# Graph network on one core: load and gather waits taken per pair of groups in the two network passes

## The reference, cut to what matters

```python
def _propagate(h, edge_attr, edge_index, We, be, Wl):
    x_i = h[edge_index[0]]
    x_j = h[edge_index[1]]
    x_edge = jnp.concatenate([x_i, x_j, edge_attr], axis=-1)
    x_edge = _mlp1(x_edge, We, be)          # silu(x @ We + be)
    x_edge = edge_attr @ Wl * x_edge
    x_p = _seg_mean(x_edge, edge_index[0], h.shape[0])
    return x_p + h
```

## Time and profile before

| | |
|---|---|
| median of 3 runs | 16204.83 us (16196.27 to 16240.02) |
| the profiled execution | 16222.93 us, its span 16221.2 us |
| POOL busy / PE busy / DVE busy | 9525.9 / 9592.5 / 7215.4 us (59% / 59% / 44%) |
| gathers of the two passes, first to last | 7210.7 to 13034.2 us |
| clock granted to TensorE, mean | 0.693 |

### The profile page before, as it was taken

The page is one execution under the profiler, slowest core; times in us unless marked ns, Lnnn a source line. Parts: engine busy times, 40 slices in busy tenths (PEclk is TensorE's granted clock), DMA queues, the critical chain, the costliest instruction groups (busy, mean ns, idle before and its releaser), DMA issues.

```text
span 16221.2 us, 180153 instructions
## 1 busy us (share of the span) xinstructions
PE 9592.5 (59%) x40895; PEld 6450.1 (40%) x40896; DVE 7215.4 (44%) x18628; ACT 3844.3 (24%) x8556; POOL 9525.9 (59%) x8465
## 2 busy tenths in 40 slices
PE   0466657766478878845555556655555545555555
PEld 0111122221133333335555554555555545555554
DVE  8876657777000000013333332333333357777776
ACT  0344444442011111112222222222222212222221
POOL 0378878888645434426666664566666645555553
PEclk9999999999688778865555555555555555555555
DMA  9922222222599989992222223222222344444444
GB/s 385 358 15 19 19 15 20 20 20 18 168 342 370 343 306 357 359 113 86 84 86 84 85 84 50 75 84 86 84 86 85 80 95 139 141 141 140 140 139 96
DMA packets 1483063, 2197.01 MB, mean 135 GB/s; under 512 B 882955, under 2 KB 926027, under 8 KB 1454669
## 3 DMA queue, kind: packets, MB, share of 16 engines
q1 hardware_dynamic: 907628, 1490.52, 28.2%
q0 software_dynamic: 453120, 343.50, 12.7%
q10 hardware_dynamic: 121698, 356.43, 6.0%
HBM read 1771.19 MB, written 419.98 MB: 135 GB/s over the span
## 4 chain that ended last, share of the span: by engine, by line
POOL 40%; DMA 22%; issue 21%; PE 8%; DVE 4%; another core or an unknown queue 3%; ACT 1%; POOLq 0%; SPq 0%; DVEq 0%; ACTq 0%
POOL gat L645 18%; POOL adj L613 12%; POOL arena L645 8%; DMA arena<-adj 8%; DMA gat<-q_table,ring_i 6%; DMA arena<-h_table,ring_i 5%; PE bank L1029 5%; DMA adj<-put_n,put_at 2%; POOL rec_src L599 1%; DVE arena L1356 1%; PE same L1161 1%; PE same L1000 1%; DVE arena L1358 1%; PE same L980 0%
## 5 line engine op out<-in xcount | busy, mean ns | idle before, releaser
L645 POOL DMA_INDIRECT gat<-q_table,ring_i x3456 | 3626.6, 1049 | 2405.7 <-DMA gat<-q_table,ring_i 1025.0
L613 POOL DMA_INDIRECT adj<-put_n,put_at x1632 | 2559.9, 1569 | 1265.3 <-DVE put_at L1440 638.1
L1183 PE MATMUL bank<-onehot_t,onehot 128*128 128x64 f32 x6912 | 1585.5, 424 | 2574.9 <-DVE acc L1578 1880.5
L1183 PEld LDWEIGHTS bank<-onehot_t,onehot 128*128 128x128 f32 x6912 | 1506.7, 330 | 2653.8 <-DVE acc L1578 1938.5
L599 POOL DMA_INDIRECT rec_src<-pay,ring_i x1632 | 1606.4, 984 | 1566.9 <-ACTq L743 1093.2
L645 POOL DMA_INDIRECT arena<-h_table,ring_i x1728 | 1729.4, 1001 | 1346.2 <-DMA arena<-h_table,ring_i 760.8
L1088 PE MATMUL same<-onehot 32*128 32x512 f16 x3264 | 1678.6, 615 | 620.0 <-DVE onehot L1411 389.3
L1029 PE MATMUL bank<-arena,hs 128*64 128x512 f32 x5880 | 1596.0, 707 | 508.2 <-DMA arena<-adj 506.9
L1419 DVE TENSOR_SCALAR_CACHE_REDUCE onehot<-same 128x128 bf16<-128x128 f32 (+3 forms) x1632 | 1233.0, 756 | 843.2 <-PE same L1090 675.9
L1173 PE MATMUL bank<-hs,arena 128*128 x6912 | 1564.0, 421 | 29.3 <-ACT arena L867 29.3
L1173 PEld LDWEIGHTS bank<-hs,arena 128*128 128x128 f32 x6912 | 1525.9, 333 | 29.8 <-issue 29.8
(11 more groups left out here) (277 smaller groups left out, 13003.2 us busy)
## 6 DMA issues: line engine op xcount, KB each, us to landing
arena<-adj SPq DMA_DIRECT2D x300, 2560.0 KB
arena<-rec_src SPq DMA_DIRECT2D x432, 552.0 KB
adj<-hs ACTq DMA_DIRECT2D x25, 6656.0 KB, 46.3
rec_src<-pay ACTq DMA_DIRECT2D x1, 119232.0 KB, 332.0
arena<-lo_row SPq DMA_DIRECT2D x432, 256.0 KB
hs<-b_row SPq DMA_DIRECT2D x108, 1024.0 KB
acc<-b_row SPq DMA_DIRECT2D x108, 1024.0 KB
gat<-q_table,ring_i POOLq DMA_INDIRECT x3456
```

Source lines behind the costliest of these rows:

```text
L613: nc.gpsimd.indirect_dma_start(counts, bass.IndirectOffsetOnAxis(put_at[:, b // 3 % 4, c:c + 1], 0), put_n[:, b // 3 % 4, c:c + 1], None, ...
L645: nc.gpsimd.indirect_dma_start(rows[n][:, u, :], None, table, bass.IndirectOffsetOnAxis(ring_i[:, n, u:u + 1], 0)).then_inc(landed[n], 16)
L1183: last = mm(bank[6 + n % 2][:, u // 2 * D:(u // 2 + 1) * D], onehot[:, n % 2, u, :], msg[n % 2][:, u, :], start=u % 2 == 0, stop=u % 2 == 1)
```

## The change

SP takes the groups of the loop in pairs (n = 0 and n = 2). Ahead of a pair it waits for three things: the gathers of the group just before the pair have landed, and `message` and `onehot_rows` of the group four before the second of the pair are through. Then it issues all four loads of the pair and increments the new semaphore `s_loaded`.

POOL, in the loop and at the first group of a pair, waits for `s_loaded` to count this pair. Its wait for the landing of the gathers before is now taken at even n only (`burst=2`); at odd n it waits for `index` alone. In the four groups written out ahead of each loop only this last part applies, as there is no wait for `s_loaded`. The attention layer calls `gathers` with `burst=1`, as before.

```diff
                 with sp.Fori(1, NG // 4) as i:
-                    for n in range(4):
-                        sp.wait_ge(l_msg, i * 4 + (k * NG + n - 3 + OFF))
-                        sp.wait_ge(l_oht, i * 4 + (k * NG + n - 3 + OFF))
+                    for n in range(0, 4, 2):
+                        hold(sp, l_gat[(n - 1) % 4], i * (16 * U) + (k * (NG // 4) + (n > 0)) * 16 * U)
+                        hold(sp, l_msg, i * 4 + (k * NG + n - 2 + OFF))
+                        hold(sp, l_oht, i * 4 + (k * NG + n - 2 + OFF))
                         load_edges(k, i, n)
+                        load_edges(k, i, n + 1)
+                        sp.sem_inc(s_loaded, 1)
...
-            def gathers(table, rows, landed, i, n, before, first):
-
-                if not first:
+            def gathers(table, rows, landed, i, n, before, first, burst=1):
+
+                if not first and n % burst == 0:
                     hold(pool, landed[(n - 1) % len(landed)], i * (16 * U) + before)
...
             def node_rows(k, i, n, first=False):
                 hold(pool, l_idx, i * 4 + (k * NG + n + 1))
-                gathers(q_table[k], gat4, l_gat, i, n, (k * (NG // 4) + (n > 0)) * 16 * U, first)
+                if not isinstance(i, int) and n % 2 == 0:
+                    hold(pool, s_loaded, i * 2 + (k * (NG // 2 - 2) + n // 2 - 1))
+                gathers(q_table[k], gat4, l_gat, i, n, (k * (NG // 4) + (n > 0)) * 16 * U, first, burst=2)
```

More of the change, by code:

```diff
@@ L368, in build @@
         l_abs = sem("l_abs")
+        s_loaded = sem("s_loaded")
         l_oht = sem("l_oht")
```

## The result

The kernel after takes 16766.37 us (median of 3 runs, 16737.46 to 16771.64) where the kernel before takes 16204.83: a ratio of 1.0343, 95% interval 1.0329 to 1.0356. The forecast was 16350 us, +145; the loss is +562. It lies outside the range of 16190 to 16560. The sign was right and the size was not.

The account below looks back on a forecast made before the run. POOL's own issue plus one landing per group was taken as the bound. Per pair 25.42 - 1.88 + 2.56 = 26.10 us; +139, +14 and -8 us sum to +145, median 16350 us, range 16190 to 16560 us.

Parts of the forecast that it names:

- Point 1: Landing gap ahead of a pair's second group shrinks from 2.18 to 0.30 us, saving 1.88 us per pair.
- Point 2: Hand-over through SP ahead of a pair's first group adds 2.56 us, bounds 2.06 and 3.46 us.
- Point 3: Gathers held by DVE's instructions move but still cost 1.65 us per pair: zero change, 0.84 us either way.
- The rival of fewer stalls: DVE's `message` and `edge_part` fall in POOL's wait for SP, 0.84 us less per pair: about 16075 us, chance 0.10.
- The closing sentence: Prediction's end: wrong if SP's loads take well under 2 us, sixteen-gather streams stall, or mean gather falls below 1.00 us.
- Point 4: PE's chain behind the late row ends about 1.9 us before DVE needs it, so it is hidden.
- the rival of the late row: Row lands beyond 7.9 us from the landing, so PE's chain sets the pair: 16517 us, chance 0.12.
- the term for the end of a pass: In a pass's last 4 pairs transfers bind, only the hand-over is added: about +1.7 us each, +14 us.
- the condition: Wrong if a second group's gathers stall with sixteen on their way; no row shows over eight not landed.

Follow-up runs that it names:

- the hand-over alone: The kernel after with `burst=1`, so that POOL takes every landing wait again: 16532.45 us, 1.0172.
- the gathers alone: The kernel before with POOL's landing wait at even groups only, SP's loads and waits as before: 16377.19 us, 1.0076.

## Why the prediction was wrong, point by point

**Point 1, the removed landing gap: right in place.** The odd groups' first gather follows at 0.30 us, and POOL's wait for landings, 195 times in the earlier trace rows, is gone from the list of waits. That this saves 1.88 us a pair assumed that the pause did nothing but pass. It let PE's reports through: by itself this half costs 126 us.

**Point 2, the hand-over: right in size, wrong on who releases it.** With full landing pauses its gap is 4.80 us, forecast 4.74. In after it is 8.4 to 8.7 us, since SP waits for `message`, not for the landing. The size is right for the pause alone; as a change of time the half was forecast at 2.56 us a pair and costs 281 us, about 1.3 us a pair, because the stalls went.

**Point 3, the stalls: mis-sized.** I took 1.65 us a pair as unchanged, with 0.84 us of play. What remains above 0.947 us is 16 x (0.969 - 0.947) = 0.35 us, a gain of 1.3 us, beyond the bound of 0.84. The rival of fewer stalls had this mechanism, also with 0.84. `message` and `onehot_columns` now run in the long pause (9035.42 to 9037.92, while POOL idles from 9032.42 to 9041.14). The closing sentence, wrong if the mean gather falls below 1.00 us, came true.

**Point 4, what becomes late: this is the step that failed.** It let every block of matmuls reach its readers 3.65 us after its start, as in the earlier trace rows, and so found 1.9 us of cover in front of the landing. `sums` of the second half of a pair is reported 10.8 us behind the end of its row, so that `onehot_columns`, `message` and with it SP's loads start late. The row itself was no trouble: L868 starts 5.0 us behind the row's issue (9010.19 to 9015.19), the 5 us that I took. So the rival of the late row, which would have set the pair by the same chain, is not what happened, though its time of 16517 us is nearer to the result.

**The sum.** Forecast 26.10 us a pair; pause 8.55 for 4.74, +3.8; stalls -1.3; that is 28.6, and 28.56 was measured. Over the passes the gathers take 6391 us for 5823 (first to last), +568 us. 204 pairs of +3.14 would be 641. The pair that I took as typical is a quick one: over 7500 to 9700 us the mean pair takes 25.74 us before and 28.68 after, +2.94. And the term for the end of a pass had the wrong sign. I put +1.7 us on each of its last pairs, without a working that gives this number; in fact the last three pairs that can be measured take 31.5 to 32.2 us each, where they took 33.6 to 35.6.

**The halves.** The right sign is in part luck. Of the two halves, one was forecast to save and costs 126 us (1.0076), the other costs 281 us (1.0172), half of what was expected of it. Together that is 2.5%, and the whole costs 3.4%. The rest arises only where both are in: SP's loads wait for `message`, `message` for late reports, and POOL for the loads. Which part of the hand-over adds it, SP's place behind `message` or POOL's wait for `s_loaded`, no run separates; the landing wait of SP does not.

I had named the condition, a second group's gathers behind sixteen not landed, as a place where no row of before spoke, but looked for its price on POOL and the transfers. The price fell on PE's signals.

## What to carry to other kernels

A pause of an engine can be work for others: before taking it away, ask what the others get done only in it, and test the removal alone before building a hand-over on it. When a wait has an unnamed releaser, compare the time at which the waiter starts with the end of the row it waits for; a gap of 10.8 us between a finished matmul and its reader is worth a question. A second reader on another engine tells in one run whether the first reader is at fault, and an increment on every matmul tells a late report from late work. Shorten such a pause by steps and at every second place; here a complete pause per two groups with a short one between gained 2.4%, and with none between it lost 0.8%.

## What the chip did that I had not expected

**Late reports of TensorE under a long gather stream.** While POOL issued indirect gathers (0.94 us every 1.25 us) without a full pause, increments from matmuls came in 2.12 us steps, and those of blocks in the second half of a stream of sixteen 10 to 14 us late, until about 1.3 us behind the last landing. In before, with eight gathers and a landing pause, none of 129 of `sums` was late, and 6 of 163 of `look_up`, by 1.0 us. But the hand-over alone has eight gathers to a stream as well, and 85 of 154 are late, by 3.1 us. Time since the last pause does not explain this either: its late `sums` rows mostly end 6.3 to 9.2 us behind the stream's start, and in before `look_up` ends 7.9 us behind it and is on time in 157 of 163. The gathers held by DVE, two per group in before and few in the hand-over alone, might break up the stream; but in the run of the gathers alone 55 of 55 blocks whose rows end 1 to 2 us behind a held gather are late all the same. What sets the moment at which the reports begin to lag is open. DVE's own increments in the kernel after came 0.01 us behind their rows, at the median and for nine in ten. The cause within the chip is open; a quarter of the gathers' bytes and eight times the increments changed nothing.

**Queues slow down too.** In the kernel with the gathers' half alone, SP's second load of a group often takes 0.70 us in place of 0.33, at a start 0.78 us behind the first in place of 0.52:

```profile
9026.78 0.33 SPq L522 DMA_DIRECT2D arena<-rec_src  x1
9027.56 0.70 SPq L523 DMA_DIRECT2D arena<-lo_row  x1
```

It is so at 73 of 330 issues of the stretch, and at none of 342 in the kernel before; in after, where SP issues in POOL's pause, at 1 of 308. Waits and register operations are slowed as well: of the rows of DVE's and PE's queues that count as no work, 41 and 29 take 0.5 to 0.95 us in after, and none in before. Whether it has the same root as the late reports was not tried.

**A held gather costs as long as its cover lasts.** The stalls of two-SBUF-operand DVE instructions, 0.10 us per gather in before, went to 0.02 us when these instructions fell into POOL's pause. The Trainium skill, SBUF — State Buffer, section Who interferes with whom, has a DVE instruction with two SBUF inputs and a GpSimd one that reads SBUF block each other; the gain of 1.3 us a pair is in line with that. The prediction took the held gathers as speaking against the same section's inference that `tensor_tensor` leaves descriptor generation alone. They need not: these gathers take their row numbers from `ring_i` in SBUF, so the reading of them may be what is held, and no run here has a gather without it.
